# One centring product for two, norm rows scaled later, and the first expert rows turned in the scores' banks

## What is computed

```python
# token mixing: attention without softmax, times a given 1024x1024 matrix
q = x @ Wq + bq;  k = x @ Wk + bk;  v = x @ Wv + bv
y = (einsum('bts,bsd->btd', d_gamma * (q @ k^T), v)) @ Wo + bo
h = where(y >= 0, y, prelu_a * y)
# a scan over time, on the layer norm of h (128 channels)
A_bar = exp(-softplus(n @ Wd + bd));  u = (1 - A_bar) * (n @ WB + bB) * (n @ Wx + bx)
state = associative scan of (A_bar, u) over the 1024 tokens
h = h + (state * (n @ WC + bC)) @ Wy + by
# experts, on the layer norm of h: the best 2 of 16 by logits, hidden 128
logits = n2 @ gate_w + gate_b;  top 2, softmax over them
h = h + sum over the two of weight * (silu(n2 @ w1[e]) * (n2 @ w2[e])) @ w3[e]
```

## Time and profile before

| | us |
|---|---|
| three runs | 329.04, 327.31, 323.82 |
| median | 327.31 |
| span of the profiled execution, first to last instruction | 331.5 |
| PE busy | 257.1 (78%) |
| DVE busy | 160.1 (48%) |
| ACT busy | 119.7 (36%) |
| POOL busy | 98.2 (30%) |

### The profile page before, as it was taken

How to read it: one execution, slowest core, us unless ns; L and a number is a source line. 1 busy time by engine, 2 the same in 40 slices (tenths; PEclk the granted TensorE clock), 3 DMA queues, 4 the chain that set the end, 5 groups by cost and what they waited for, 6 DMA issues and landing times.

```text
span 331.5 us, 4678 instructions
## 1 busy us (share of the span) xinstructions
PE 257.1 (78%) x1645; PEld 156.7 (47%) x1645; DVE 160.1 (48%) x283; ACT 119.7 (36%) x283; POOL 98.2 (30%) x119
## 2 busy tenths in 40 slices
PE   8999999988935976258829995169964899952995
PEld 7443332532411323136529884168642698621563
DVE  1453649789805993167705610053410466710664
ACT  1302561764108711467534541022320344311341
POOL 4000000004760077303771047600476000674000
PEclk9999999999985999658965997555796599995699
DMA  7999800000111101332221675995121323021101
GB/s 191 371 388 278 170 0 0 4 0 12 40 51 57 33 20 52 89 95 73 55 58 44 154 160 131 209 222 114 41 59 28 83 65 78 19 44 20 34 16 32
DMA packets 45990, 29.74 MB, mean 90 GB/s; under 512 B 32688, under 2 KB 41072, under 8 KB 45456
## 3 DMA queue, kind: packets, MB, share of 16 engines
q1 hardware_dynamic: 30416, 23.15, 27.1%
q10 hardware_dynamic: 12480, 3.15, 4.3%
q0 software_dynamic: 3072, 3.15, 3.9%
HBM read 20.46 MB, written 8.98 MB: 89 GB/s over the span
## 4 chain that ended last, share of the span: by engine, by line
PE 52%; another core or an unknown queue 19%; ACT 11%; DVE 10%; issue 7%; ACTq 0%; POOL 0%; DVEq 0%; POOLq 0%
PE ring L1013 10%; PE ring L971 9%; PE turn L988 7%; PE side L1025 5%; PE acc L816 4%; PE ring L802 4%; ACT squares L611 3%; PE side L843 3%; DVE mixed L1141 2%; PE ring L759 2%; PE side L775 2%; ACT n L629 2%; PE acc L934 1%; DVE state L1190 1%
## 5 line engine op out<-in xcount | busy, mean ns | idle before, releaser
L559 POOL DMA_INDIRECT slots<-n,slot_i x48 | 47.8, 996 | 121.9 <-DVE slot_i L1256 108.2
L1283 DVE TENSOR_TENSOR act<-ring,silu 128x512 f32<-128x512 f32 x56 | 38.4, 690 | 89.5 <-ACT silu L681 68.6
L569 POOL DMA_INDIRECT back_v<-results,slot_i x48 | 46.5, 968 | 81.4 <-DMA results<-res 67.7
L681 ACT ACTIVATE silu<-ring 128x512 f32<-128x512 f32 x56 | 33.3, 597 | 78.7 <-remote 38.5
L1141 DVE TENSOR_TENSOR mixed<-ring,dg 128x1024 f32<-128x1024 f32 x32 | 38.6, 1218 | 19.5 <-remote 10.9
L816 PE MATMUL acc<-mixed,v 128*64 128x512 f32 x128 | 34.3, 628 | 8.6 <-DVE mixed L1141 8.4
L802 PE MATMUL ring<-kq 64*128 64x512 f32 x128 | 33.5, 629 | 0.0
L1013 PE MATMUL ring<-nT,w_sb 64*128 64x256 f32 x128 | 24.2, 459 | 8.8 <-issue 8.0
L971 PE MATMUL ring<-slots_t,w_shared 64*128 64x128 f32 x192 | 19.8, 328 | 13.7 <-issue 12.7
L988 PE MATMUL turn<-w_sb,act 128*128 128x64 f32 (+1 forms) x192 | 29.1, 314 | 0.0
L988 PEld LDWEIGHTS turn<-w_sb,act 128*128 128x128 f32 x192 | 27.3, 226 | 3.0 <-issue 2.2
(11 more groups left out here) (150 smaller groups left out, 306.5 us busy)
## 6 DMA issues: line engine op xcount, KB each, us to landing
dg<-dgT SPq DMA_DIRECT2D x8, 512.0 KB, 7.8
dg<-given SPq DMA_DIRECT2D x8, 512.0 KB, 15.7
slots<-zeros SPq DMA_DIRECT2D x3, 1024.0 KB, 13.2
w_shared<-w SPq DMA_DIRECT2D x48, 64.0 KB, 2.2
slots<-slots SPq DMA_DIRECT2D x12, 256.0 KB
results<-res ACTq DMA_DIRECT2D x12, 256.0 KB, 2.9
w_sb<-w SPq DMA_DIRECT2D x2, 1024.0 KB, 14.3
xs<-xT SPq DMA_DIRECT2D x4, 256.0 KB, 6.5
```

The source lines that it names most:

```text
L559: pool.indirect_dma_start(out=slots_dram[r], out_offset=bass.IndirectOffsetOnAxis(ap=slot_i[:, r, k, i:i + 1], axis=0), in_=n2[:, u % 2, i ...
L569: pool.indirect_dma_start(out=back_v[:, r, i, k, :], out_offset=None, in_=results_dram[r], in_offset=bass.IndirectOffsetOnAxis(ap=slot_i[: ...
L681: s.activation(silu[:, n % 2], hidden_banks(n)[:, :, 0:PAIRS * P], ACT.Silu).then_inc(silu_done, 1)
L1283: dve.tensor_tensor(act[:, n % ACT_BUFS], hidden_banks(n)[:, :, PAIRS * P:2 * PAIRS * P], silu[:, n % 2], ALU.mult).then_inc(act_done, 1)
```

## The change

- **Start.** 30 small warm-up products instead of 50, and none of the other 20. K of the first half is projected ahead of the product of wvo. The DMAs of `vec` and `wvo` are issued by ACT instead of SP. V's second half, K1 and Q1 move from ahead of the beats to beat 2.
- **One centring product.** `center_m` and `gate_w` lie side by side in one tile `cg`, so `center2` is four products of 160 columns over both banks of `side`, where it was four of 128 and four of 32. `take_raw` and `take_logits` read that layout, the latter in two instructions. `turn_h` now also waits for the logits.
- **Scaled rows** of the second norm are issued behind the next unit's squares and square root, where they stood ahead.
- **Places** move one beat on, behind the first product with drive for units 0 and 1 (in unit 2 they keep their place ahead of it).
- **First slots** are turned into ring's banks 0 and 1 as soon as the scores of step 30 are read. Expert work begins at beat 62 instead of 65, with other rates; by the end of the beats 32 pieces are issued, where it was 28. Fifth shared weights are loaded behind the second slot load instead of ahead of the first.

```diff
-    "center2": (16, 17), "turn_h": (21, 17), "count": (24, 21), "owner_row": (27, 14), "prelu": (0, 0),
+    "center2": (16, 17), "turn_h": (21, 19), "count": (24, 21), "owner_row": (28, 14), "prelu": (0, 0),
...
-    "logits": (19, 18), "mark0": (19, 19), "one0": (22, 19), "mark1": (22, 20), "one1": (22, 21), "place": (25, 24),
-    "slots": (25, 24), "spread": (25, 27), "owners": (30, 35), "weights": (24, 22), "dispatch": (4, 22),
+    "logits": (19, 18), "mark0": (19, 19), "one0": (22, 19), "mark1": (22, 20), "one1": (22, 21), "place": (26, 24),
+    "slots": (26, 24), "spread": (26, 27), "owners": (31, 35), "weights": (24, 22), "dispatch": (4, 22),
...
-WEIGHTS_AFTER = (-2, -2, -2, -2, -1, 3, 3, 6, 7, 7, 9, 11)
+WEIGHTS_AFTER = (-2, -2, -2, -2, 1, 3, 3, 6, 7, 7, 9, 11)
...
-FFN_BEAT = 65
+FFN_BEAT = 62
...
-WARM = 50
-WARM2 = 20
+WARM = 30
...
+        def slots_bank(i):
+            return ring[:, i, :] if i < 2 else acc[:, :]
...
+            s.dma_start(vec[:, :], vecs).then_inc(ld_vec, 16)
+            s.dma_start(wvo_sb, wvo).then_inc(ld_wvo, 16)
...
-                for u in due("rows2", m):
-                    if u < LAST:
-                        scale_rows(u)
                 for u in due("relu", m):
...
                 for u in due("std1", m):
                     norm_std(0, u)
+                for u in due("rows2", m):
+                    if u < LAST:
+                        scale_rows(u)
...
             def center2(u):
                 pe.wait_ge(hT2_done, u + 1)
                 for t in range(TT):
-                    mm = pe.matmul(side[:, 1, t * P:(t + 1) * P], hT[:, u % 2, t * P:(t + 1) * P], center_m[:, :],
+                    mm = pe.matmul(side[:, t // 2, t % 2 * CG:(t % 2 + 1) * CG], hT[:, u % 2, t * P:(t + 1) * P], cg[:, :],
                                    start=True, stop=True)
                 mm.then_inc(cen_done[1], 1)
-                for t in range(TT):
-                    mm = pe.matmul(side[:, 0, t * 2 * NE:(t + 1) * 2 * NE], hT[:, u % 2, t * P:(t + 1) * P], gate_w[:, :],
-                                   start=True, stop=True)
-                mm.then_inc(raw_done, 1)
 
             def turn_h(u):
                 pe.wait_ge(raw_taken, u + 1)
+                pe.wait_ge(logits_done, u + 1)
...
             def turn_slots(i):
                 if i == 0:
+                    pe.wait_ge(mixed_done, ALL_STEPS - 1)
+                if i == 2:
                     pe.wait_ge(relu_done, 2 * UNITS)
...
             warm_up(WARM)
+            project_kq(0, "K0")
             pe.wait_ge(ld_wvo, 16)
...
-            warm_up(WARM2)
-            project_kq(0, "K0")
             project_kq(0, "Q0")
             project_v(0, 0)
             scores(0)
-            project_v(0, 1)
-            project_kq(0, "K1")
-            project_kq(0, "Q1")
-            pe.wait_ge(consts, 1)
```

More of the change, by code:

```diff
@@ L67 @@
 VW, VB, VO, VCOLS = 0, 128, 256, 320
+CG = P + 2 * NE
 BEAT = {
@@ L235, in build_layer @@
         wgate_sb = sb("wgate_sb", [P, 2 * NE])
-        gate_w = sb("gate_w", [P, 2 * NE])
+        cg = sb("cg", [P, CG])
+        center_m, gate_w = cg[:, 0:P], cg[:, P:CG]
         wv = sb("wv", [P, P])
@@ L252, in build_layer @@
         ident = sb("ident", [P, P])
-        center_m = sb("center_m", [P, P])
         before = sb("before", [P, P], BF16)
@@ L378, in turned_sum, with cg_tiles @@
             return side[:, 1, 0:GB * D]
+        def cg_tiles():
+            return side[:, :, 0:2 * CG].rearrange("p k (t c) -> p k t c", c=CG)
         def count_bank(u):
@@ L952, in hidden @@
                     pe.wait_ge(ld_w12, 32)
+                    pe.wait_ge(sin_done, 2)
+                if n == 1 and q == 0:
                     pe.wait_ge(mixed_done, ALL_STEPS)
@@ L1204, in take_logits @@
             def take_logits(u):
-                dve.wait_ge(raw_done, u + 1)
+                dve.wait_ge(cen_done[1], u + 1)
                 dve.wait_ge(scale_done, u + 1)
-                raw = side[:, 0, 0:UT * NE].rearrange("p (i e) -> p i e", e=NE)
-                link(dve.tensor_tensor(logits[:, :, :], raw, stats[:, 1, 2, :].unsqueeze(2).broadcast_to([P, UT, NE]), ALU.mult))
+                for k in range(2):
+                    i = slice(k * UT // 2, (k + 1) * UT // 2)
+                    raw = cg_tiles()[:, k, :, P:CG].rearrange("p t (b e) -> p t b e", b=BH)
+                    scale = stats[:, 1, 2, i].rearrange("p (t b) -> p t b", b=BH).unsqueeze(3).broadcast_to([P, UT // 4, BH, NE])
+                    link(dve.tensor_tensor(logits[:, i, :].rearrange("p (t b) e -> p t b e", b=BH), raw, scale, ALU.mult))
                 dve.tensor_tensor(logits[:, :, :], logits[:, :, :], row_of(row, UT), ALU.add).then_inc(logits_done, 1)
```

25 lines of the change are left out of this document (15 added, 10 removed).

## The result

The changed kernel is clearly slower, by about 25 us. The prediction had added 4.8 us. Executions of one kernel fall into a faster and a slower group, the slower one at a lower granted clock, and the ratios with an interval are those on record for the faster group.

A forecast was written before the change was run, and what follows sets the result against it. PE was taken to bound the kernel through most of the program. Terms -2.5 + 0.4 + 4.1 + 5.8 + 3.0 - 6.0 = +4.8 us, put on the median 327.31, gave 332 us; range 326 to 338, wide 318 to 341.

The forecast's parts named there:

- start: Start of the program: fewer small warm-up products on PE bring the first scores sooner; -2.5 us, ends 1.5 and 3.0.
- middle beats: Middle token units: later row scaling and places, logits scaled in two instructions; +0.2 us for each of two units, +0.4.
- keep, to the last ReLU: Unit 2: ACT computes keep only behind the copy of turned rows, so the scan starts later; +4.1 us.
- last unit's ACT chain: Last ReLU to transposed norm: four more table loads and two SiLUs on ACT, one slot copy less; +5.8 us.
- count of unit 2: Unit 2's count product on PE waits until ACT has read the experts' results from its bank; +3.0 us, ends 0 and 4.
- count to last centring: From unit 2's count product to the last unit's centring product; the sum had no term here, 0.
- centring to pair 4: Last centring product to expert pair 4: PE has one pair more of hidden products done; -6.0 us, ends 0 and -10.3.
- behind pair 4: From PE's product of expert pair 4 to the end: order the same in both kernels, so 0.
- the list of signs: What the profile after should show, among it keep near 121 and centring to pair 4 about 15 us.
- the pair ahead: Seven hidden products instead of five done at the last centring product, one pair more, worth 5.14 us, taken as -6.0.
- The slower one: Rival: pair ahead worth little, as the last unit's turned h also waits for the logits; +10.8, 338 us; chance 0.33.
- The faster one: Rival: the 14.1 us of stops fall under queued expert products or don't come; 318 us; under 10 to pair 4; chance 0.19.

The follow-up runs named there:

- late_again: The changed kernel with the early experts undone (beat 65, old rates, old slot turning and weight loading); 262.0 us, ratio 1.000 to the kernel before.
- after_third: The changed kernel, unchanged, run on a chip without stops; 283.3 us beside 258.8 for the kernel before, ratio 1.101.
- after_again: The changed kernel, unchanged, run again on a chip with stops; 356.3 us beside 330.0 for the kernel before, ratio 1.085.
- before_again: The kernel before, unchanged, run again for a profile on a chip with stops; 335.2 us in one run.
- given_free: The changed kernel with the dense experts' broadcast read from an input and issued two slot loads earlier; 345.3 us, ratio 1.050 to the kernel before.
- before_clean: The kernel before, unchanged, meant as a profile without stops but run on a chip with them; 333.5 us in one run.

## Why the prediction was wrong

Step by step, on the chip of the prediction (before to after) and, as a second witness without stops, late_again to after_third:

| step | said | measured | without stops |
|---|---|---|---|
| start | -2.5 | -0.9 | +1.5 |
| middle beats | +0.4 | +0.4 | +0.4 |
| keep, to the last ReLU | +4.1 | +5.4 | +5.1 |
| last unit's ACT chain | +5.8 | +6.9 | +7.0 |
| count of unit 2 | +3.0 | +3.0 | +3.1 |
| count to last centring | 0 | +3.1 | +3.7 |
| centring to pair 4 | -6.0 | -11.4 | -5.0 |
| behind pair 4 | 0 | +10.1 | +3.8 |

Each measured value is the change of one interval: first scores 10.23 to 9.28, last scores 121.53 to 121.00, last ReLU 126.90 to 131.80, norm 145.91 to 157.73, count 150.27 to 165.12, centring 164.80 to 182.72, pair 4 185.46 to 192.03. In the last column both kernels have the new start and middle, so its first two entries are what two executions of one order differ by.

**What held.** Keep's place, the five table loads, the wait of the count and, within 1.3 us each, their sizes. Keep starts at 123.14, near the 123.9 of the sum's working; the 121 in the list of signs did not fit that working. No gap follows a table load: the one at 145.39 ends at 146.67, and the square root starts at 146.68. None stands ahead of one either: the square root ends at 155.94, and the next load starts at 155.96. The drain that the Trainium skill (ScalarE: Activation LUTs, "What ACT_TABLE_LOAD costs") adds to each switch is not in the rows after either, so the trace decides against it. Up to pair 4 the sum said +4.8 and the profile has +6.6, but that nearness is luck: 3.1 us between count and centring that the sum had at nothing met 5.4 us more gain behind the centring than it had. The same stretch from centring to pair 4 took 17.7 us in after_again (178.51 to 196.23), with two stops in it, 9.07 and 3.67 us, and not 9.3; in before_again it took 21.1. Without stops the terms from keep to pair 4 sum to +14.0, where the prediction had +6.9.

**The step that failed.** It is the sentence "The order behind that point is the same in both kernels, so the question is when PE gets there." The sum had everything behind pair 4 at 0 by it, and 10.1 us of the miss are there. The order was the same, but two things are awaited behind that point which don't come sooner when PE gets there sooner: the routing weights of the last unit, at which PE stood 3.26 us where it had not stood before, and their broadcast, whose issue hung on where a stop falls. DVE waited 9.38 us for it where it had not waited for it before, and given_free, without the wait for the broadcast, is 11.0 us faster than the changed kernel beside it. My rows of before could have warned me: a stop of 17 us lay over the broadcast, and I had read the stops as a loss, not as a cover.

This also sizes the term of -6.0 for the pair ahead. It was taken at pair 4, and most of what is won there is waited out again: without stops 5.0 us are won there and 3.26 go at the routing weights. From the last centring product to the end of the program the kernel before takes 166.7 us (164.80 to 331.5) and the one after 165.5 (182.72 to 348.2), late_again 112.9 and after_third 111.6. So the pair ahead is worth 1.2 us at the end in both comparisons, and what stands in front of the centring product, 17.9 us of delay with stops and 20.8 without, is paid almost in full. With stops single executions differ by more than that: after_again has 173.0 us there, beside 168.0 and 166.9 in before_again and before_clean, so there it was worth nothing.

**Sizes.** The start won 0.9 and not 2.5. 50 small products took 4.60 us before and 30 take 3.38, 113 ns each; so the first 30 were the slow ones, and the 20 removed took 1.22 us together, 61 ns each, not 1.84. K0's two products then took 2.02 us, where four took 1.94 before, and those of wvo 0.4 us more (6.35 to 7.33, before 5.76 to 6.35): they now came while PE still ran at its slow pace. 1.22 + 1.12 - 1.05 - 0.39 is 0.9. This part differs between executions: in the 14 traces with the new start K0's two products take from 1.08 to 2.05 us and the first scores start at 7.75 to 9.28; in the 6 with the old one they start at 9.87 to 11.36. By the medians, 8.5 and 10.4, the start is worth some 1.9 us. Keep cost 3.4 us at the scan where 4.1 was said, but PE, idle for 4 us, did the output product in 1.97 us instead of 1.08, at a granted clock of 0.50, which is 1.2 GHz. The row of the windows, with columns as in the earlier trace rows:

```profile
128.00:132.00 4.00, 3.93 (x9) 1.04 (x10) 2.30 (x5) 0.20 (x1) 3.08 (x4) 0.50 0.09 31
```

**The rest of the miss** is the base. The sum was made against the span of 331.5, which is 4.3 above the median of the times before; the span after is 3.9 below the median of its own. Of the 20.1 us by which 352.1 misses 332, 1.8 lie up to pair 4, 10.1 behind it, and 8.2 in this, that one profiled execution was high among its runs and the other low.

**The rivals.** The slower one was right in its direction and near in its price: it had the pair ahead worth nothing, and to the end it was worth 1.2 us. Its reason is half of the one seen. It had the turned h in front of pair 4 wait for the logits, and in after_third PE does stand there, 1.35 us for the logits; the longer wait, 3.26 us for the routing weights that are made from them, comes behind the pair. Its 338 us still lie 14 below the 352.1. The faster one is out, although its sign came: 9.3 us from the last centring product to pair 4, under the 10 that I had named for it. after_again has 17.7 there, so that sign told of where a stop fell. The remote starts of ACT from the last ReLU to pair 4 sum to 10.0 us (7.79 and 2.19). For before I had counted four, 14.1 us, and passed over two more in the same stretch, 2.41 us at 160.86 and 1.66 at 177.85, so 18.2 in all.

## What to carry to other kernels

Here work that was moved ahead of a serial chain, on the engines that the chain uses, was paid for at once, and most of what it brought was waited out at the next things that hung on that chain. So read behind the last moved instruction too: name each transfer that is awaited there, what covers it now, and whether the cover moves with it, since a stall that looks like a loss can be the cover of a load. And check one profile's span against the runs before a sum is put on a median.

## What the runs showed that was not expected

The same program took 258 us on some chips and 327 to 331 on others, and 68 us of it went away there with POOL's indirect DMAs. A store of 256 KB, 3.5 us in the median, took 22.6 us beside a broadcast of 4 MB from another queue; in another kernel two executions, one with such a wait of 7.53 us and one without, differ by 7.2. And in the first microseconds PE's products ran at half their later pace (113 and 61 ns for a small one, 1.01 us for one of K0's where the four of K0 and Q0 took 0.49 each before), although the granted clock reads 1.00 in the windows from 2 to 6 us.
